# A four-stage post-norm network on one core: the experts' product in halves with small transposes moved, and two pairs of banks with later transposes at the transformer's entry

## What is computed

```python
x = _layernorm(x + _L0_attn_ref(x, ...), axis=-1)   # state-space layer: conv, softplus, scan
x = _layernorm(x + _L0_ffn_ref(x, ...), axis=-1)    # experts
x = _layernorm(x + _L1_attn_ref(x, ...), axis=-1)   # second state-space layer
x = _layernorm(x + _L1_ffn_ref(x, ...), axis=-1)    # transformer, 6 layers
```

```python
def _moe_linear(x, router_w, expert_w):      # 8 experts, top 2
    logits = x @ router_w.T
    vals, idx = jax.lax.top_k(logits, K)
    probs = jax.nn.softmax(vals, axis=-1)
    ...
    for e in range(n_exp):
        out = out + combine[:, e:e + 1] * (x @ expert_w[e].T)
    return out
g = _moe_linear(xt, router_gate, w_gate)     # 128 -> 512
u = _moe_linear(xt, router_up, w_up)         # 128 -> 512
inter = jax.nn.silu(g) * u
d = _moe_linear(inter, router_down, w_down)  # 512 -> 128
```

```python
for i in range(DEPTH):
    x = attn_layer(shift_tokens(x), Wqkv[i], q_scale[i], k_scale[i], Wo[i]) + x
    x = ffn_layer(shift_tokens(x), ln_g[i], ln_b[i], W1[i], b1[i], W2[i], b2[i]) + x
```

## Time and profile before

| | us |
|---|---|
| median of 3 runs | 4295.19 (4294.84 to 4295.83) |
| the profiled execution's own time | 4293.15 |
| its span, first to last instruction | 4291.4 |
| PE busy | 4099.0 (96% of the span) |
| DVE busy | 3322.2 (77%) |
| ACT busy | 2405.5 (56%) |
| POOL busy | 2222.5 (52%) |
| mean granted PE clock | 0.980 of full speed |

### The profile page before, as it was taken

One profiled execution on the slowest core, in us unless ns is written; L12 is line 12 of the kernel. 1 busy time (PEld: TensorE's weight loads), 2 busy tenths in 40 slices (PEclk: granted clock), 3 DMA queues, 4 the chain that ended last, 5 costly groups with the idle time before them and its releaser, 6 DMA issues.

```text
span 4291.4 us, 144514 instructions
## 1 busy us (share of the span) xinstructions
PE 4099.0 (96%) x63655; PEld 2977.7 (69%) x63655; DVE 3322.2 (77%) x6991; ACT 2405.5 (56%) x4362; POOL 2222.5 (52%) x1342
## 2 busy tenths in 40 slices
PE   4999999976899999999999999999999999999997
PEld 3776677663677777777777777777777777777775
DVE  5444443454888888888988889888898888889995
ACT  1010011043667767776777677766777677766664
POOL 1101000014666666666666666666666666666662
PEclk8999999997999999999999999999999999999998
DMA  4111111000111111111111111111111111111110
GB/s 153 41 40 60 40 40 60 21 1 11 37 40 37 41 50 50 38 41 36 50 52 40 36 36 55 47 41 36 40 57 46 36 40 42 55 42 39 44 38 27
DMA packets 76231, 186.16 MB, mean 43 GB/s; under 512 B 15819, under 2 KB 44630, under 8 KB 71126
## 3 DMA queue, kind: packets, MB, share of 16 engines
q1 hardware_dynamic: 75606, 176.91, 13.4%
HBM read 61.25 MB, written 2.36 MB: 15 GB/s over the span
## 4 chain that ended last, share of the span: by engine, by line
PE 65%; DVE 5%; ACT 3%; issue 1%; POOL 1%; DVEq 0%; POOLq 0%
PE pQ L1635 15%; PE pS L1619 9%; PE pM L1701 7%; PE pO L1679 7%; PE pM L1690 7%; PE pC L1735 6%; PE pO L1666 5%; PE pT L1666 4%; PE pT L1647 3%; PE pC L1745 3%; ACT sq L1504 2%; ACT pS L1488 1%; DVE rot L1354 1%; DVE m L1358 1%; DVE n L1369 1%
## 5 line engine op out<-in xcount | busy, mean ns | idle before, releaser
L1272 POOL TENSOR_TENSOR rot<-rot,m 128x1024 f32<-128x1024 f32 x384 | 906.5, 2361 | 397.2 <-DVE m L1358 397.2
L1264 POOL TENSOR_TENSOR rot<-rot,rn 128x1024 f32<-128x1024 f32 x384 | 733.8, 1911 | 280.6 <-DVE rn L102 280.6
L1504 ACT ACTIVATE sq<-pQ 128x1024 f32<-128x1024 f32 x384 | 394.2, 1027 | 457.6 <-PE pQ L1635 457.3
L1281 POOL TENSOR_TENSOR E<-E,rc 128x512 f32<-128x512 f32 x384 | 401.2, 1045 | 344.2 <-DVE rc L1344 344.1
L1354 DVE TENSOR_TENSOR rot<-pQ,tabl 128x1024 f32<-128x1024 f32 x384 | 461.7, 1202 | 36.7 <-ACT sq L1504 36.2
L1358 DVE TENSOR_TENSOR m<-pQ,tabl 128x1024 f32<-128x1024 f32 x384 | 466.1, 1214 | 0.0
L1666 PEld LDWEIGHTS pO<-PT,V 64*64 64x64 f32 x12288 | 389.3, 135 | 109.4 <-issue 100.7
L1369 DVE TENSOR_REDUCE n<-sq 128x16 f32<-128x1024 f32 x384 | 464.0, 1208 | 0.0
L1619 PEld LDWEIGHTS pS<-kT,qT 64*32 64x32 f32 x24576 | 362.0, 107 | 138.2 <-issue 103.1
L1619 PE MATMUL pS<-kT,qT 64*32 64x64 f32 x24576 | 426.4, 218 | 22.3 <-issue 12.4
L570 POOL TENSOR_TENSOR b_xcT<-b_cB,b_xT 128x2048 f32<-128x2048 f32 x16 | 72.1, 4505 | 709.3 <-DMA b_cB<-b_crow 665.1
(11 more groups left out here) (224 smaller groups left out, 7564.4 us busy)
## 6 DMA issues: line engine op xcount, KB each, us to landing
V<-V SPq DMA_DIRECT2D x192, 384.0 KB, 3.5
b_cB<-b_crow SPq DMA_DIRECT2D x32, 1024.0 KB, 5.8
xs<-XT SPq DMA_DIRECT2D x192, 64.0 KB, 2.9
V<-V SPq DMA_DIRECT2D x96, 128.0 KB, 3.3
ys<-XT SPq DMA_DIRECT2D x192, 64.0 KB, 2.1
wq<-in_wqkv SPq DMA_DIRECT2D x6, 512.0 KB, 4.9
wk<-in_wqkv SPq DMA_DIRECT2D x6, 512.0 KB, 4.2
wv<-in_wqkv SPq DMA_DIRECT2D x6, 512.0 KB, 5.5
```

Of the source, the lines that this page charges most:

```text
L1264: e.tensor_tensor(r, r, rn[b % 2][:, c:c + HEADS].unsqueeze(2).to_broadcast([P, HEADS, HD]), ALU.mult)\
L1272: e.tensor_tensor(rot[j % RING][:, :], rot[j % RING][:, :], m2[:, :, :].rearrange("p h d -> p (h d)"), ALU.add)\
L1504: e.activation(sq[:, :], pQ[:, :], ACT.Square).then_inc(a_sq.sem, 1)
```

## The change

In `moe_phase`: the product `it` is made in two instructions of 512 columns, each waiting for its half of the up product (`pm_` and `vm` get a step more); `r_ct` moves behind the up product and writes into the free half of `pm[1]`; the transposes of `X` for the next sequence (`r_xt(n + 1)`) follow it, ahead of `m_ld`, rather than opening the next pass; `m_ld` waits also for ACT's copy of `cT`, which reads the same bank.

```diff
                 if M:
                     m, p = M
                     e.wait_ge(am_.sem, am_.at("sig", m))
-                    e.wait_ge(pm_.sem, pm_.at("u", m))
-                    e.tensor_tensor(it[:, :, :].rearrange("p c l -> p (c l)"), pu[:, :], sig[:, :], ALU.mult).then_inc(vm.sem, 1)
+                    for b in range(2):
+                        half = slice(b * 512, (b + 1) * 512)
+                        e.wait_ge(pm_.sem, pm_.at("u", m, 1 - b))
+                        e.tensor_tensor(it[:, 2 * b:2 * b + 2, :].rearrange("p c l -> p (c l)"), pu[:, half], sig[:, half], ALU.mult)\
+                            .then_inc(vm.sem, 1)
...
-                def r_xt():
-                    if R:
-                        n, p = R
-                        if later(n):
-                            e.wait_ge(ar.sem, ar.at("ctc", n - 1))
+                def r_xt(n):
+                    if n < NSEQ:
+                        if n:
+                            e.wait_ge(ar.sem, ar.at("xT", n - 1))
...
                         e.wait_ge(vm.sem, vm.at("gu", m))
+                        if R:
+                            e.wait_ge(ar.sem, ar.at("ctc", R[0]))
...
-                r_xt()
+                if R and R[0] == 0:
+                    r_xt(0)
                 m_experts(0, 0, 1)
                 r_lg()
                 m_experts(0, 1, 4)
-                m_experts(1, 0, 2)
+                m_experts(1, 0, 4)
                 r_ct()
-                m_experts(1, 2, 4)
+                if R:
+                    r_xt(R[0] + 1)
                 m_ld()
```

```diff
+        projected = lambda j: pTO if j < 8 and j % 2 else pQ
+        squared = lambda j: E2[:, :, :].rearrange("p a k -> p (a k)") if j < 8 and j % 2 else sq[:, :]
+        before = lambda j: j - 2 if j <= 8 else j - 1
...
-                if j:
-                    e.wait_ge(v_rot.sem, v_rot.at("sin", j - 1))
+                if before(j) >= 0:
+                    e.wait_ge(v_rot.sem, v_rot.at("sin", before(j)))
                 for i in range(2):
-                    x = e.matmul(pQ[:, i * 512:(i + 1) * 512], xs[n % 3][:, t * P:(t + 1) * P], wqkv[w][:, i * 512:(i + 1) * 512],
+                    x = e.matmul(projected(j)[:, i * 512:(i + 1) * 512], xs[n % 3][:, t * P:(t + 1) * P], wqkv[w][:, i * 512:(i + 1) * 512],
                                  start=True, stop=True)
                 x.then_inc(p_q.sem, 1)
+                if j + 1 < NSEQ:
+                    take(j + 1)
```

More of the change, by code:

```diff
@@ L673, in run @@
                         e.wait_ge(gr.sem, gr.at("xu", n - 1))
-                    e.activation(cT[:, :], pm[0][0:2 * NE, 0:L], ACT.Copy).then_inc(ar.sem, 1)
+                    e.activation(cT[:, :], pm[1][0:2 * NE, L:2 * L], ACT.Copy).then_inc(ar.sem, 1)
                 if M:
@@ L709, in r_ct @@
                         for t in range(T):
-                            m = e.transpose(pm[0][0:2 * NE, t * P:(t + 1) * P], cb[:, 2 * t:2 * t + 2, :].rearrange("p j n -> p (j n)"),
+                            m = e.transpose(pm[1][0:2 * NE, L + t * P:L + (t + 1) * P], cb[:, 2 * t:2 * t + 2, :].rearrange("p j n -> p (j n)"),
                                             ident[:, :])
@@ L731, in m_experts @@
                                                 start=x == 0, stop=x == NE - 1)
-                            if j == CF - 1 or (r == 0 and j == 1):
+                            if j % 2:
                                 last.then_inc(pm_.sem, 1)
@@ L1120, in transformer_phase @@
         rc = sb("rc", [P, NG, NW])
-        E = [sb(f"E{i}", [P, NW * KEYS]) for i in range(2)]
+        E2 = sb("E2", [P, 2, NW * KEYS])
+        E = [E2[:, i, :] for i in range(2)]
         PT = [sb(f"PT{i}", [P, NW * KEYS]) for i in range(2)]
@@ L1368, in squares @@
                     e.wait_ge(v_nt.sem, v_nt.at("rs", n))
-                e.tensor_reduce(n2[:, c:c + HEADS], sq[:, :].rearrange("p (h d) -> p h d", d=HD), AX.X, ALU.add)\
+                e.tensor_reduce(n2[:, c:c + HEADS], squared(j).rearrange("p (h d) -> p h d", d=HD), AX.X, ALU.add)\
                     .then_inc(v_red.sem, 1)
@@ L1473, in _, with taken @@
         def _(e):
-            for s in range(NSEQ):
+            def taken(s):
                 e.wait_ge(p_in.sem, p_in.at("xt", s))
                 e.activation(XT[:, s, :], pM[s % 2][:, 0:L], ACT.Copy).then_inc(a_in.sem, 1)
+            taken(0)
             e.wait_ge(const_l, 64)
@@ L1501, in square @@
                 e.wait_ge(p_q.sem, p_q.at("q", j))
-                if j:
-                    e.wait_ge(v_red.sem, v_red.at("rd", j - 1))
-                e.activation(sq[:, :], pQ[:, :], ACT.Square).then_inc(a_sq.sem, 1)
+                if before(j) >= 0:
+                    e.wait_ge(v_red.sem, v_red.at("rd", before(j)))
+                e.activation(squared(j), projected(j)[:, :], ACT.Square).then_inc(a_sq.sem, 1)
+                if j + 1 < NSEQ:
+                    taken(j + 1)
             def probs(n, g):
@@ L1590, in _, with take @@
             e.transpose(pC[:, 0:DEPTH], b2r[:, :], ident[0:DEPTH, 0:DEPTH]).then_inc(p_b2, 1)
-            for s in range(NSEQ):
-                if s >= 2:
-                    e.wait_ge(a_in.sem, a_in.at("xt", s - 2))
+            def take(s):
+                if bank[s % 2]:
+                    free(s % 2)
                 for t in range(T):
@@ L1597, in _, with free @@
                 bank[s % 2] = (a_in, "xt", s)
+            def free(i):
+                st, step, n = bank[i]
+                e.wait_ge(st.sem, st.at(step, n))
+            take(0)
             e.wait_ge(v_set, 1)
```

15 lines of the change are left out of this document (6 added, 9 removed).

## The result

| | before | after |
|---|---|---|
| median, us | 4295.51 of 4 runs (4294.84 to 4301.35) | 4261.91 of 4 runs (4261.47 to 4263.29) |
| the profiled execution's own time | 4293.15 | 4261.88 |
| its span | 4291.4 | 4260.1 |
| PE busy | 4099.0 | 4080.9 |
| mean granted PE clock | 0.980 | 0.985 |

The ratio is 0.9923, with a 95% interval from 0.991 to 0.9935: 33.6 us faster, where 37 were forecast (4258 us, range 4247 to 4273). In the changed kernel's numbering L741 is L745, L752 is L756, L730 is L732, L627 is L629, L636 is L639, L674 is L677; in the transformer L1595 is L1609, L1635 is L1650, L1354 is L1364, L1619 is L1634, L1679 (the output projection of the attention) is L1696.

What follows compares the result with a forecast made beforehand. PE was taken as the bound, busy 96% of the span. From 4293.15 us, experts -27.0 and entry -10.1 gave 4256.1, or 4258 us against the median; range 4247 to 4273.

Steps and rivals of the forecast that it cites:

- Product in halves: Experts: DVE's second half takes 0.692 us against 1.23, so L741 starts 0.53 us earlier in 16 passes: -8.5 us.
- Transposes moved: Experts: 15 `r_ct` and 14 `r_xt` leave PE's path and lie in the wait before L741: -6.4 us.
- The clock: Experts: down products into `b_pg` slowed by the lower PE clock drop from 12 of 16 to 4: -13.6 us.
- falls as often: Rival: the clock falls in 12 of 16 experts passes as before, the 13.6 us are missing: 4272 us, chance 0.08.
- never falls: Rival: the clock falls in no experts pass, 7 us more gained: 4251 us, chance 0.09.
- Transposes don't hold the clock: Rival: in the experts' wait, transposes keep the clock up no better than idle time; 7 or 8 falls, 4264 us, chance 0.13.
- The chain behind `r_ct`: Experts: cT's copy, write, reads and POOL's xu come later, xg waits for POOL with 0.4 us slack: +1.5 us.
- the rival on the slower side: Experts: L612 too waits for POOL, PE stands 2.7 us in each of 15 passes: 4312 us, chance 0.04.
- The entry: Transformer's start: earlier first projection, two pairs of banks and later transposes together give -10.1 us (ends -4 and -15).
- Start: Entry: first projection starts at 1011.5 rather than 1016.55 us, DVE's first L1354 at 1016.4 against 1019.59: -3.2 us.
- First pass: Entry: with two pairs of banks, DVE's first to fifth L1354 takes 18.3 us instead of 28.2: -9.9 us.
- the long rest keeps its 3183 us: Transformer from 1108 us on: instructions left alone by the change, PE busy 3135 of 3183 us, no change in time.

Runs made afterwards that it cites:

- halves_only: Only the product made in halves, transposes and banks as in the kernel before; against the kernel before: 4269.6 us, ratio 0.9943.
- moe_only: The changed kernel's experts phase with the transformer phase of the kernel before; against the kernel before: 4270.3 us, ratio 0.9946.
- moved_only: Only the experts' transposes moved, the product left in one piece; against the kernel before: 4284.7 us, ratio 0.9977.

## Why the prediction was right

By its steps:

1. *Product in halves, -8.5:* right; measured -10.1 (wait 22.6 to 12.5). The half takes 0.69 us as read from another line of the same size.
2. *Transposes moved, -6.4:* right in kind, -4.9 (halves_only against moe_only, 702.2 to 698.5, with one fall and 2.9 us of late xg set off). It is shown by traces alone; the medians of the two kernels are 4269.6 and 4270.3 us. The copy, thought to end just within the wait with 0.04 us of cover, ends 0.16 us ahead of L745 in the pass shown.
3. *The clock, -13.6:* right. 4 falls were forecast; 3 and 5 came, in further profiles of the changed part 3, 4, 4 and 5: 12 to 15 us. The rivals "falls as often" and "never falls" are out. "Transposes don't hold the clock" named 7 or 8 falls, which did not come; but halves_only, with the same 0.78 us and nothing in them, fell 6 times, so the distance that tells the two apart is 6 against 3 to 5 falls, and 12 against 9 in moved_only.
4. *The chain behind `r_ct`, +1.5:* the mechanism was right, the size too small: +2.6 to +6.1 us. In six profiles with the changed experts part 10 to 13 of 16 xg took over 2.5 us. The step reckoned xg's end against the gate product with a slack of 0.4 us and POOL's start at L + 8.4, 1 us either way; it started between L + 8.1 and L + 11.6. Behind a down product at full clock, each start beyond L + 9.1 costs PE the rest (a start at 9.58 cost 0.51, one at 10.64 cost 1.57), so the slack was 0.3 larger than reckoned and the landing up to 3.2 us late. halves_only, where the chain isn't moved, has xg at 2.28 us throughout. L612 stays at 0.35 us, so the rival on the slower side is out.
5. to 8. *The entry, -10.1:* right, -10 to -11. Start: -3.2 forecast, -3.4 measured for DVE's first product, but -1.6 against the second profile of the kernel before, whose clock rose earlier. First pass: 18.3 us forecast, 18.55 measured. Second pass (fifth L1354 to the scores): +2.5 forecast, +2.2 measured (26.6 to 28.8 us). The fifteen transposes between: +0.5 forecast; from the scores to the first output projection the changed kernel takes 42.7 us where 43.0 were, so this cost does not show.

The experts come to -27.4 in the profile against -27.0, but the two kernels' profiles differ there by 24 to 31 us, so that the hit to half a microsecond is luck; the usual miss is step 4. The assumption "the long rest keeps its 3183 us" was right to about a microsecond on average and wrong for this profile, by 7 us. It had no term in the range, and it should have had one.

## What to carry to other kernels

Halving the last elementwise instruction in front of a matmul pays twice where the clock falls behind the wait: in halves_only half of the 20 us came from the clock. Before instructions are moved later past a long product, follow the whole chain behind them to the next point where two engines read SBUF together; here DVE had 3.5 idle us ahead of that point, and using them gave back what the step had cost. And before a loss in an untouched part is explained, profile the same program twice.

## What the runs showed that was not expected

- PE stops, mostly for 0.65 to 1.3 us, in front of the scores about every 13 passes, and goes on 1.15 to 1.61 us behind the landing of a packet of instructions. 128 waits more ahead of the phase moved all but the last of the stops by three passes. They cost 12 to 18 us of the 3140 in every kernel here.
- One program's long part differs by up to 7 us from execution to execution (3137.6 and 3144.6), with PE's idle time and the granted clock both taking part.
- In the kernel before, POOL's xu also held DVE's cast L588 (2.18 us in the pass of the earlier trace rows, against 0.17 to 0.18 for this cast in the changed kernel, where xu starts later). It stood on no path.
